# Self-attention on one core: keys interleaved over the partitions, each flipped block moved by four transfers of its own

## The reference

```python
# x: (4, 128, 32, 32); 4 groups of 32 channels
y = ((xg - mu) * rsqrt(var + EPS)).reshape(B, C, H, W) * gamma + beta
qkv = einsum('bchw,dc->bdhw', y, w_qkv) + b_qkv          # q, k, v: (B, C, N), N = 1024
scores = einsum('bnc,bcm->bnm', q, k) * C ** (-0.5)
w = softmax(scores, axis=-1)
a = einsum('bnm,bmc->bnc', w, v)
out = einsum('bchw,dc->bdhw', a, w_out) + b_out
return x + out
```

## Time and profile before

| | |
|---|---|
| median of 3 runs | 145.96 us (144.68 to 146.13) |
| span of the profiled execution, first to last instruction | 143.7 us |
| TensorE busy | 133.6 us, 93% |
| VectorE busy | 103.9 us, 72% |
| ScalarE busy | 67.7 us, 47% |
| GpSimd busy | 57.1 us, 40% |
| data moved by transfers | 15.07 MB in 6154 packets |

### The profile page before, as it was taken

The page is one execution under the profiler, slowest core; times in us unless marked ns, Lnnn a source line. Parts: engine busy times, 40 slices in busy tenths (PEclk is TensorE's granted clock), DMA queues, the critical chain, the costliest instruction groups (busy, mean ns, idle before and its releaser), DMA issues.

```text
span 143.7 us, 1862 instructions
## 1 busy us (share of the span) xinstructions
PE 133.6 (93%) x589; PEld 94.4 (66%) x589; DVE 103.9 (72%) x201; ACT 67.7 (47%) x122; POOL 57.1 (40%) x66
## 2 busy tenths in 40 slices
PE   7999999997499979997999999999999999999990
PEld 7978579873367635665655556766776666768770
DVE  0597587799978999899496987898763787463402
ACT  3164858763266526543361364455843666353000
POOL 6032347963334666633355556433543213330000
PEclk9999999999999999999999999999999999999998
DMA  4940000000045976983598539973996001000211
GB/s 159 310 188 0 0 5 0 0 2 0 0 101 117 206 165 141 206 200 109 109 203 197 152 66 206 206 182 81 212 203 168 0 0 73 0 0 0 80 70 73
DMA packets 6154, 15.07 MB, mean 105 GB/s; under 512 B 1664, under 2 KB 1664, under 8 KB 6144
## 3 DMA queue, kind: packets, MB, share of 16 engines
q1 hardware_dynamic: 5856, 14.69, 41.3%
q10 hardware_dynamic: 288, 0.27, 0.5%
HBM read 2.36 MB, written 2.10 MB: 31 GB/s over the span
## 4 chain that ended last, share of the span: by engine, by line
PE 66%; DVE 14%; SPq 7%; issue 5%; ACT 4%; DMA 2%; DVEq 0%
PE mixed L765 22%; SPq L235 7%; PE scores L715 5%; PE scores L714 5%; PE turned L731 5%; PE scores L717 5%; DVE scores L527 5%; PE scores L773 4%; DVE crossed L552 4%; ACT probs L366 3%; PE mixed L760 3%; PE mixed L762 3%; PE mixed L761 3%; PE turned L661 2%; PE mixed L661 2%
## 5 line engine op out<-in xcount | busy, mean ns | idle before, releaser
L295 POOL TENSOR_SCALAR probs<-probs,inv_sum 128x1024 f32<-128x1024 f32 x32 | 35.9, 1122 | 63.7 <-DVE inv_sum L532 63.7
L527 DVE TENSOR_SCALAR_CACHE_REDUCE scores<-scores,key_bias 128x1024 f32<-128x1024 f32 x31 | 40.0, 1289 | 13.9 <-PE scores L717 13.8
L366 ACT ACTIVATE probs<-scores,neg_max 128x1024 f32<-128x1024 f32 x32 | 35.7, 1115 | 18.7 <-DVE scores L527 17.7
L765 PE MATMUL mixed<-crossed,v 128*128 128x512 f32 x80 | 37.7, 593 | 1.0 <-DMA crossed<-crossed 1.0
L714 PE MATMUL scores<-y_hi,z_hi 128*128 128x512 f32 x62 | 34.6, 558 | 0.3 <-DVE z_lo L489 0.3
L552 DVE STREAM_TRANSPOSE crossed<-probs 128x1024 f32<-128x1024 f32 x20 | 24.8, 1241 | 0.0
L715 PE MATMUL scores<-y_lo,z_hi 128*128 128x512 f32 x62 | 24.4, 394 | 0.0
L765 PEld LDWEIGHTS mixed<-crossed,v 128*128 128x128 f32 x80 | 14.1, 190 | 11.6 <-issue 11.0
L717 PE MATMUL scores<-y_hi,z_lo 128*128 128x512 f32 x62 | 19.3, 392 | 0.0
L714 PEld LDWEIGHTS scores<-y_hi,z_hi 128*128 128x128 f32 x62 | 11.7, 189 | 8.8 <-issue 5.7
L715 PEld LDWEIGHTS scores<-y_lo,z_hi 128*128 128x128 f32 x62 | 11.7, 189 | 7.0 <-issue 5.5
(11 more groups left out here) (147 smaller groups left out, 168.9 us busy)
## 6 DMA issues: line engine op xcount, KB each, us to landing
crossed<-crossed SPq DMA_DIRECT2D x80, 128.0 KB, 2.3
out_dram<-result SPq DMA_DIRECT2D x8, 256.0 KB, 2.5
xs<-in_x_dram SPq DMA_DIRECT2D x2, 512.0 KB, 6.4
xs<-in_x_dram SPq DMA_DIRECT2D x3, 256.0 KB, 5.0
xs<-in_x_dram ACTq DMA_DIRECT2D x1, 256.0 KB, 3.5
ws<-in_weights_dram SPq DMA_DIRECT2D x1, 256.0 KB, 3.7
vecs<-in_vectors_dram ACTq DMA_DIRECT2D x1, 3.0 KB, 3.9
```

What stands on the lines that cost most here:

```text
L295: pool.tensor_scalar(probs[:, i % RING, :], probs[:, i % RING, :], inv_sum[:, i:i + 1], 1.0, ALU.mult, ALU.mult).then_inc(s_probs, 1)
L366: act.activation(probs[:, i % RING, :], scores[:, i % 2, :], ACT.Exp, bias=neg_max[:, i:i + 1], scale=-1.0, accum_out=row_sum[:, i:i + 1]) ...
L527: dve.tensor_scalar(scores[:, i % 2, :], scores[:, i % 2, :], key_bias[:, b % 2, i:i + 1], None, ALU.subtract, ALU.min, accum_out=neg_max[ ...
L765: mm = pe.matmul(bank, v[:, b % 2, k, :], at, start=first, stop=final)
```

## The change

Every block is now flipped by VectorE; TensorE turns nothing, and the split into high and low parts for groups 6 and 7 is gone, so all groups mix in fp32. A flipped block is moved by four transfers right after its flip. Each takes 32 partitions of the flipped block, cuts each row into four pieces of 256 elements, and lays them on 128 partitions: partition 4c + t instead of 32t + c. So keys come out interleaved over the partitions, and the values must stand in the same order: y, from which values are projected, is written with its columns permuted (by_partition), on GpSimd with every fourth element. The key biases come out of that projection permuted as well, so they are copied, turned back by a matmul with a permutation matrix, and then biased. For batch 0 a plain y_first serves scores and key biases (first_key_bias, single columns), and first_y_moved makes the permuted one; its value jobs move from the front and slots 0 and 1 to slots 2, 3 and 4.

The jobs of the next batch are ordered V0, Z0, V1, V2, Z1 in slots 3 to 7, all in the `turned` banks; statistics move to slots 2 and 3; the mix table is two tiles a slot from slot 4g + 5 on; results come at slot 4g + 9; the last group is mixed in two halves of 256 queries, each with its own result and store. The core of the diff:

```diff
-    Z0, V0, V1, Z1, V2 = range(JOBS)
-    JOB_SLOT = {4: Z0, 5: V0, 6: V1, 7: Z1}
+    V0, Z0, V1, V2, Z1 = range(JOBS)
+    JOB_SLOT = {3: V0, 4: Z0, 5: V1, 6: V2, 7: Z1}
+    UNPERMUTE_SLOT = {4: V0, 6: V1, 7: V2}
+    FIRST_V = {2: V0, 3: V1, 4: V2}
...
+    for group in range(GROUPS_OF_FOUR - 1):
+        for k in range(QB):
+            MIX.setdefault(QB * group + 5 + k, []).append((group, 2))
...
+        flipped = sb("flipped", [128, FLIPS, N])
+        home = sb("home", [128, HOMES, SQ, QB, N // SQ])
...
+        def by_tile(columns):
+            return columns.rearrange("p (v t c) -> p v t c", t=SQ, c=32)
+        def by_partition(columns):
+            return columns.rearrange("p (v c t) -> p v t c", t=SQ, c=32)
...
+            def move(n):
+                group = n // QB
+                sp.wait_ge(s_flipped, n + 1)
+                if n % QB == 0 and group >= HOMES:
+                    sp.wait_ge(s_mixed, KT * (group - HOMES + 1))
+                for g in (0, 2, 1, 3):
+                    sp.dma_start(home[:, group % HOMES, g, n % QB, :],
+                                 flipped[32 * g:32 * g + 32, n % FLIPS, :].rearrange("c (t x) -> c t x", t=SQ)
+                                 ).then_inc(s_landed[n % FLIPS], 16)
...
+            for n in range(BATCHES * BLOCKS):
+                move(n)
+                if n >= 11 and n % QB == 3:
+                    store((n - 11) // QB)
...
+                pool.tensor_scalar(by_partition(y[:, b % 2, :]), by_tile(xs[:, b, :]), norm_a[:, b:b + 1],
+                                   norm_b[:, b:b + 1], ALU.mult, ALU.add).then_inc(s_y, 1)
+            def first_y_moved():
+                pool.tensor_scalar(by_partition(y[:, 0, :]), by_tile(xs[:, 0, :]), norm_a[:, 0:1],
+                                   norm_b[:, 0:1], ALU.mult, ALU.add).then_inc(s_y_moved, 1)
...
+                    if b == 0 and i == 1:
+                        first_y_moved()
                     if i == (0 if b == 0 else 1) and b + 1 < BATCHES:
                         normalised_input(b + 1)
...
-                    if not swapped(BLOCKS * b + i):
-                        turned_copy(BLOCKS * b + i)
-                    if b == 0 and i in (0, 1):
-                        first_values((V1, V2)[i], mixed[:, i, :])
+                    if b == 0 and i in FIRST_V:
+                        first_values(FIRST_V[i], mixed[:, i % 2, :])
                     if i in JOB_SLOT and not last:
                         projection_copy(b + 1, JOB_SLOT[i], turned[:, JOB_BANK[JOB_SLOT[i]], :])
                     if after(b, i, 2)[0] < BATCHES:
                         exponentials(*after(b, i, 2))
...
             coefficients(1, 2, 2, mixed[:, 0, MINUS_MEAN + 1:MINUS_MEAN + 2])
+            flip(0)
...
                         maximum(*ahead)
-                    if not swapped(BLOCKS * b + i):
-                        turned_copy(BLOCKS * b + i)
-                    if swapped(BLOCKS * b + i + 1):
+                    if BLOCKS * b + i + 1 < BATCHES * BLOCKS:
                         flip(BLOCKS * b + i + 1)
+                    if i in UNPERMUTE_SLOT and not last:
+                        key_biases(b + 1, UNPERMUTE_SLOT[i], turned[:, JOB_BANK[UNPERMUTE_SLOT[i]], :])
...
-                    if b + 2 < BATCHES and i in (4, 5):
-                        half_stats(b + 2, i - 4)
-                        if i == 5:
+                    if b + 2 < BATCHES and i in (2, 3):
+                        half_stats(b + 2, i - 2)
+                        if i == 3:
                             channel_stats(b + 2, b + 3)
...
+            def first_values(job, bank):
+                if job == V0:
+                    pe.wait_ge(s_norm, 2)
+                    pe.wait_ge(s_y_moved, 1)
...
+            def key_bias_back(b, job, bank):
+                lo, hi = V_TILES[job]
+                pe.wait_ge(s_key_bias_moved, unpermuted(b, job))
+                pe.wait_ge(s_v, 3 * b + V_NO[job] + 1)
...
+                pe.matmul(bank[:, KEY_BIAS:KEY_BIAS + hi - lo], permute[:, :], key_bias_moved[:, lo:hi],
+                          start=True, stop=True).then_inc(s_key_bias_back, 1)
...
+            def mix_tile(bank, group, k, blocks):
+                b = group // HALVES
+                at = home[:, group % HOMES, :, blocks, k * 32:(k + 1) * 32].rearrange("p g u r -> p u g r")
+                pe.matmul(bank, v[:, b % 2, k, :], at, start=k == 0, stop=k == KT - 1).then_inc(s_mixed, 1)
...
-            values(0, V0, turned[:, 1, :]).then_inc(s_v0, 1)
+            first_key_bias(0, 2)
...
-            mix(GROUPS_OF_FOUR - 1, KT)
+            for group, count in MIX[BATCHES * BLOCKS]:
+                mix(group, count)
+            pe.wait_ge(s_result, GROUPS_OF_FOUR - 2)
+            last_mix(mixed[:, 1, 0:QUARTER], slice(0, 2))
+            pe.wait_ge(s_key_bias, unpermuted(BATCHES - 1, V2))
+            last_mix(turned[:, 0, 0:QUARTER], slice(2, QB))
```

More of the change, by code:

```diff
@@ L44, in attention_kernel @@
     GROUPS_OF_FOUR = BATCHES * HALVES
[L45 to L53, removed]
+    FLIPS = 4
+    HOMES = 3
+    MOVED = 16 * SQ
+    MIX = {}
+    for group in range(GROUPS_OF_FOUR - 1):
+        for k in range(QB):
+            MIX.setdefault(QB * group + 5 + k, []).append((group, 2))
     x_v = x.rearrange("b c h w -> b c (h w)")
@@ L195, in job_count, with unpermuted @@
             return JOBS * (b - 1) + job + 1
[L197 to L216, removed]
+        def by_tile(columns):
+            return columns.rearrange("p (v t c) -> p v t c", t=SQ, c=32)
+        def by_partition(columns):
+            return columns.rearrange("p (v c t) -> p v t c", t=SQ, c=32)
+        def unpermuted(b, job):
+            return 3 * (b - 1) + V_NO[job] + 1
         @block_ctx.sync
@@ L590, in _ @@
             dve.wait_ge(s_y0_hi, 2)
[L591 removed]
+            dve.tensor_tensor(y_lo[:, 0, pieces[1]], y_first[:, pieces[1]], y_hi[:, 0, pieces[1]].bitcast(fp32),
                               ALU.subtract).then_inc(s_y0_lo, 1)
@@ L641, in _ @@
             results(GROUPS_OF_FOUR - 2)
-            results(GROUPS_OF_FOUR - 1)
+            last_results(0, mixed[:, 1, 0:QUARTER])
+            last_results(1, turned[:, 0, 0:QUARTER])
         @block_ctx.tensor
@@ L837, in _ @@
                         block_scores(*ahead)
-                    if b == 0 and i == 0:
-                        pe.wait_ge(s_key_bias, 1)
-                    if not swapped(BLOCKS * b + i):
-                        turn(BLOCKS * b + i)
-                    if b == 0 and i == 0:
-                        pe.wait_ge(s_norm, 2)
-                        values(0, V1, mixed[:, 0, :]).then_inc(s_v0, 1)
-                    if b == 0 and i == 1:
-                        pe.wait_ge(s_z0_lo, 3)
-                        values(0, V2, mixed[:, 1, :]).then_inc(s_v0, 1)
-                    if i == 0 and b > 0:
-                        projection(b, V2, mixed[:, 1, :])
+                    if b == 0 and i in FIRST_V:
+                        first_values(FIRST_V[i], mixed[:, i % 2, :])
+                    if i in UNPERMUTE_SLOT and not last:
+                        job = UNPERMUTE_SLOT[i]
+                        key_bias_back(b + 1, job, turned[:, JOB_BANK[job], :])
                     if i in JOB_SLOT and not last:
```

272 lines of the change are left out of this document (112 added, 160 removed).

## The result

| | before | after |
|---|---|---|
| median of the runs, us | 145.33 | 148.37 |
| lowest to highest, us | 144.68 to 146.13 | 147.28 to 148.99 |
| span of the profiled execution, us | 143.7 | 146.5 |
| mean granted clock in it | 0.997 | 0.965 |

The ratio of the changed kernel's time to that of the kernel before is 1.0195, with a 95% interval of 1.0114 to 1.0276: slower, by 1 to 3%. I had forecast 145.8, no change; the time lies in the range of 142.0 to 149.8, but on the slower side.

What follows compares the result with a forecast made beforehand. TensorE was taken as the bound from scores(10), waits before it: 49.5 + 88.8 + 0.9 = 139.2 us for its end, span 142.2, 143.5 with the clock, 145.8 with 2.3 carried over; range 142 to 149.8.

Steps and rivals of the forecast that it cites:

- The walk through the front: Slots 0 to 7: waits followed in order, putting scores(10) at 49.5 us instead of 42.6, 6.9 lost.
- The strided step: GpSimd's y writing every fourth element: 1.8 us taken, between 1.19 and 2.56; first_y_moved ends at 28.75.
- The clock's price: TensorE falls from 2.4 to 1.2 GHz in the front: 1.3 us taken, bounded by nothing and 5.3.
- the gaps were longer: Front: TensorE's idle gaps, 3.2 and 4.6 us, exceed the earlier 2.6 at full clock, so the clock falls.
- Rival (3): Front: clock at half through slot 4 and into the first mixes, 5.3 us instead of 1.3, 149.8 us; chance 0.20.
- I take 0.9 us of waits in all: TensorE behind scores(10): only each batch's first turned-back key bias comes late, by 0.4 us; 0.9 in all.
- the last landing: Tail: block 31's last transfer lands at 135.4 us, when group 7's first half ends at 135.8, so just hidden.
- the 88.8: TensorE's work from scores(10) on: 81.9 us plus 6.9 for group 7.
- rival (4): Transfers: 1 KB pieces cost over 0.11 us and become the bound, 158 us; chance 0.08.
- (1): Front: clock and stride cost nothing, -1.3 and -1.2 us, so 143.3 us; chance 0.20.
- (2): Front: the first value job's copy does not delay exp(4), max(5) 3.3 us earlier, about 142.5 us; chance 0.10.
- The carry from span to time: End of the sum: 2.3 us, runs' median minus profiled span, added to the 143.5 us span, giving 145.8.

Runs made afterwards that it cites:

- warm_front: Changed kernel plus 11 and 21 score-sized matmuls that nothing reads in TensorE's idle time of slots 1 and 2: 145.97 us, ratio 1.0023 to the kernel before.
- first_y_early_halves: Changed kernel with first_y_moved ahead of the first normalisation, batch 0's value jobs in slots 0 to 2, later batches' y in two halves: 142.14 us, ratio 0.9774.
- y_halves: Changed kernel with each next batch's y in two operations of 512 columns, the first value job waiting for the first alone: 146.37 us, ratio 1.0073.
- contiguous_y: Changed kernel with GpSimd writing y in plain column order, so values no longer match the keys' order: 145.27 us, ratio 0.9982 to the kernel before.
- v0_after_scores5: Changed kernel with batch 0's first value job moved from slot 2 to slot 3, behind scores(5): 145.95 us, ratio 0.9967 to the kernel before.

## Why the prediction was wrong, by its own steps

The walk through the front named each wait and its order correctly; two of its sizes were too small. Behind scores(10) the waits of the same step, in later batches, were missing from the sum.

| step | predicted | measured |
|---|---|---|
| max(2), max(4) | 20.1, 25.5 | 20.10, 25.51 |
| first_y_moved ends | 28.75 | 29.40 |
| exp(4) starts | 30.2 | 31.59 |
| max(5) | 32.1 | 33.86 |
| max(8) | 43.1 | 45.77 |
| scores(10), without and with 1.3 for the clock | 49.5, 50.8 | 51.70 |
| TensorE's end, with the clock | 140.5 | 143.55 |
| span | 143.5 | 146.5 |

- **The strided step** was the first term mis-sized: 1.8 us taken between 1.19 and 2.56, measured 2.20 and 2.16. Twice in a row on GpSimd this makes first_y_moved 0.65 us late.
- **The clock's price** was the second: 1.3 us taken, 1.9 measured (warm_front), so 0.6 short. That it would fall in this front was right, but partly by luck: the gap behind which it fell was 2.69 us, not 3.2, hardly more than the 2.60 that had left it at 1.00, and in first_y_early_halves it fell behind 2.04. My reason, that the gaps were longer, does not carry it. It came back only at 34, behind V1. Rival (3), with the full 5.3, did not come: scores(6) ran at full clock, and the price stayed under the 2.9 from which I let it decide. The walk's own times are without the clock; 0.65 and 1.9 are nearly all of the 2.7 by which max(8) came later. Up to scores(10) 0.5 came back (5.9 us instead of 6.4), so that 0.9 us of the miss lie ahead of it.
- **The larger part of the miss, 2.2 us, lies behind scores(10)**: 91.9 us instead of 89.7. The step that failed is "I take 0.9 us of waits in all": it stood for a key bias that comes too late. I priced the strided y on the front alone and did not follow it into slots 9 to 11 of the later batches, so its waits were put at nothing. In slot 11 norm_b ended at 61.25 us, y ran from 61.36 to 63.56, and TensorE, idle for 0.76 when V0 started at 63.70, had been ready since 62.94. A plain step of 1.19 would have ended at 62.55, in time; the strided one did not. Two such waits cost 1.84 us from start to start (y_halves), and the last landing, "just hidden" by 0.4, was 0.39 late: 2.2 us of waits. The key bias that the 0.9 stood for did not wait at all; in y_halves, with V0 on time, it waits once, 0.4 late as foretold, and so the halves win 1.4 us. Waits thus make 1.3 us of the 2.2. The rest, some 0.8, is work above the 88.8: a half of z took 0.78 us (67.70 to 68.48) instead of 0.70, a V0 0.75 (63.70 to 64.45) instead of 0.67; I have not assigned all of it.
- **Its largest terms were right**: slots of two tiles and one block's scores took 3.10 us (3.12 by the sum), and the result to the end 2.9 as predicted. The move's issue and landing hid as foretold: rival (4), the transfers as bound, is out.
- **Rivals (1) and (2)** each asked for what the runs gave only when it was taken out by hand: no stride 145.3, full clock 146.0; first_y_moved out of the way 141.9. My argument against (2), the order of norm(3) on GpSimd, was true of the change as made. I had looked at where the step stood and not at where GpSimd was idle before.
- **The Trainium skill**, GPSIMD Engine Reference, section 7 (Performance pitfalls for Q7 kernels), says that reads in steps over 8 bytes cost half as much again. The runs differ from it: the two-input tail of y rose from 1.28 to 1.53 us, a fifth, and the one-input step from 1.19 to 2.19 with a strided read, by 84%. The measurement decides.
- **The carry from span to time** was a small slip: I added 2.3 us, the distance of the runs' median from the profiled span. Where one execution gives both, they are 1.8 apart (148.32 and 146.5).

## What to carry to other kernels

When a change makes one operation slower, follow it to every place where its result is waited for, in the later rounds of the loop as in the first, and ask there by how much it was early. Before sizing a new operation's wait, look for an idle stretch of its engine from which its inputs are already there: the same 2.2 us step cost some 6 us at one place in GpSimd's order, the clock's price included, and nothing at another. And where the new wait idles TensorE, its clock is a price of its own: here a slot or two at half clock was worth 2 us, and 32 matmuls that nothing reads kept it. A wait that is taken out can also uncover the next one: read the path again, from start to start, and not only the bracket that went.

## What the runs showed of the hardware

- An fp32 step of GpSimd over 128x1024 takes 1.19 us in sequence (contiguous_y) and 2.13 to 2.22 with a stride, the same for a strided write by 4 elements and a strided read by 32. I had expected the two sides to differ. In two halves it takes 1.27 each, 2.44 for both as they overlap a little (y_halves), so cutting it costs little.
- The granted clock held behind an idle stretch of 1.81 us in one kernel and fell behind one of 2.04 us at the same place in another, and the clock of one kernel differed from run to run (0.965 to 1.00 in v0_after_scores5). Before, it held over 2.6 us. What else decides was not settled.
